# Moving fill parts, row-maximum scores and denominators between the steps of an attention stage, and one DMA ahead in a queue

## The reference, cut to what matters

```
B, T, D = x.shape                       # 2, 1024, 512; H = 16 heads, d = 32
q1, q2 = split(x @ Wq1), split(x @ Wq2)
k,  v  = split(x @ Wk),  split(x @ Wv)
q  = concatenate([q1, q2], axis=1)      # 32 query heads over 16 key heads
scores = einsum('bhqd,bhkd->bhqk', q, repeat(k, 2)) / sqrt(d)
scores = where(causal, scores, finfo.min)
p  = softmax(scores)
y  = einsum('bhqk,bhkd->bhqd', p, repeat(v, 2))
y1, y2 = y[:, :H], y[:, H:]
y  = y1 - sigmoid(x @ Wlam) * y2
return y.reshape(B, T, D) @ Wo
```

## Time and profile before

| what | us |
|---|---|
| median of 3 runs (2035.85 to 2036.71) | 2036.25 |
| the profiled execution, its own time | 2035.62 |
| its span, first to last instruction | 2033.8 |
| TensorE busy | 1964.0 |
| VectorE busy | 1304.9 |
| GpSimd busy | 864.2 |
| ScalarE busy | 827.8 |

### The profile page before, as it was taken

One profiled execution on the slowest core, in us unless ns is written; L12 is line 12 of the kernel. 1 busy time (PEld: TensorE's weight loads), 2 busy tenths in 40 slices (PEclk: granted clock), 3 DMA queues, 4 the chain that ended last, 5 costly groups with the idle time before them and its releaser, 6 DMA issues.

```text
span 2033.8 us, 36873 instructions
## 1 busy us (share of the span) xinstructions
PE 1964.0 (97%) x15184; PEld 834.6 (41%) x15184; DVE 1304.9 (64%) x2610; ACT 827.8 (41%) x1259; POOL 864.2 (42%) x451
## 2 busy tenths in 40 slices
PE   7998999899999999999999999999998899899999
PEld 3444444444444443333333333333333334344444
DVE  5868686836847456566666666666667635774644
ACT  4435353425444322444444443444434452543431
POOL 3756575800000000667767677777776740000000
PEclk9999999999999999999999999999999999999999
DMA  8111010030000003000101000010000211000001
GB/s 243 32 31 35 28 42 27 21 140 1 1 1 1 1 8 70 23 17 23 22 21 24 12 24 16 22 23 22 2 23 6 62 34 42 1 1 22 21 1 42
DMA packets 71592, 60.21 MB, mean 30 GB/s; under 512 B 37312, under 2 KB 55744, under 8 KB 71168
## 3 DMA queue, kind: packets, MB, share of 16 engines
q1 hardware_dynamic: 64512, 45.27, 7.8%
q10 hardware_dynamic: 6912, 12.59, 2.1%
HBM read 43.02 MB, written 10.62 MB: 26 GB/s over the span
## 4 chain that ended last, share of the span: by engine, by line
PE 53%; DVE 5%; POOL 2%; issue 1%; ACT 1%; DMA 0%; SPq 0%; DVEq 0%; POOLq 0%; ACTq 0%
PE psum L128 9%; PE psum L1231 8%; PE psum L1321 8%; PE psum L1379 6%; PE psum L1362 6%; PE psum L152 5%; PE psum L1271 3%; PE psum L1335 2%; PE psum L1358 2%; POOL b_totals L1628 1%; PE psum L1349 1%; DVE b_maxima L1701 1%; PE psum L1280 1%; DVE psum L1709 1%; DVE x L1767 0%
## 5 line engine op out<-in xcount | busy, mean ns | idle before, releaser
L1628 POOL TENSOR_TENSOR b_totals<-b_totals,b_probs 128x2048 f32<-128x2048 f32 (+3 forms) x100 | 323.9, 3239 | 151.3 <-ACT b_probs L1546 147.7
L1709 DVE CUSTOM_DVE_ANT_0 psum<-psum,b_rest 128x512 f32<-128x512 f32 (+3 forms) x512 | 233.5, 525 | 173.4 <-PE psum L1321 173.3
L447 PE MATMUL psum<-hT,a_win 128*128 128x512 f32 x640 | 292.5, 600 | 0.8 <-ACT hT L574 0.8
L128 PE MATMUL psum<-hT,b_early 128*128 128x512 f16 x1024 | 227.0, 381 | 9.8 <-DVE b_middle L214 6.9
L128 PE MATMUL psum<-hT,W 128*128 128x512 f16 x1024 | 227.5, 382 | 3.6 <-DVE a_win L214 3.6
L1546 ACT ACTIVATE b_probs<-psum 128x1024 f32<-128x1024 f32 (+3 forms) x214 | 153.6, 768 | 150.9 <-PE psum L1362 150.8
L1701 DVE TENSOR_REDUCE b_maxima<-psum 128x2 f32<-128x1024 f32 x128 | 150.8, 1220 | 85.5 <-PE psum L1321 85.2
L1628 POOL TENSOR_TENSOR b_totals<-b_totals,b_rest 128x2048 f32<-128x2048 f32 (+3 forms) x50 | 162.0, 3240 | 68.3 <-ACT b_rest L1546 66.5
L447 PEld LDWEIGHTS psum<-hT,a_win 128*128 128x128 f32 x640 | 120.1, 192 | 130.4 <-issue 129.2
L128 PEld LDWEIGHTS psum<-hT,b_early 128*128 128x128 bf16 x1024 | 99.9, 98 | 133.6 <-DVE b_middle L214 8.8
L128 PEld LDWEIGHTS psum<-hT,W 128*128 128x128 bf16 x1024 | 100.7, 99 | 126.3 <-issue 7.0
(11 more groups left out here) (244 smaller groups left out, 3429.5 us busy)
## 6 DMA issues: line engine op xcount, KB each, us to landing
a_parts<-in_w_guT ACTq DMA_DIRECT2D x32, 256.0 KB, 2.8
ternary<-W SPq DMA_DIRECT2D x1, 6144.0 KB, 18.2
a_win<-in_w_inT SPq DMA_DIRECT2D x20, 256.0 KB, 7.2
a_parts<-in_w_pT ACTq DMA_DIRECT2D x16, 256.0 KB, 2.6
b_down<-lam_rows SPq DMA_DIRECT2D x32, 128.0 KB, 2.7
b_early<-ternary SPq DMA_DIRECT2D x8, 512.0 KB, 8.6
out<-x SPq DMA_DIRECT2D x16, 256.0 KB, 2.6
x<-in_x SPq DMA_DIRECT2D x3, 1024.0 KB, 7.9
```

What stands on the lines that cost most here:

```text
L128: last = pe.matmul(self.bank[self.up_bank(i, m) + part], self.gu[:, k * 2 * HID + col:k * 2 * HID + col + P], self.hT[:, at:at + BLK], sta ...
L447: last = pe.matmul(ring(s, j), win[:, at:at + P], core["hT"][:, (i * KT + k) * BLK:(i * KT + k + 1) * BLK], start=(k == 0), stop=(k == KT ...
L1628: pool.tensor_tensor(acc, acc, held(u, s)[:, :, off:BLK], ALU.add).then_inc(summed, 1)
L1709: last = dve.tensor_tensor_reduce(scores, scores, row_mask[:, BLK - width:BLK], 1.0, -3e38, ALU.add, ALU.max, maxima[u % 2][:, at:at + 1])
```

## The change

- A step has three places, of which place 0 always comes ahead of `row`, and 1 and 2 behind it. The parts of a job are listed one by one, so they need not be neighbours.
- `FIRST_ROW` is 0: the nine portions of `row` are at steps 0 to 8, and their order is another.
- Key and query parts stand at (0,1) to (3,2); the second projection's parts from (4,1) to (8,2). Both `den` come at place 0, of steps 2 and 4 (before: behind the row of steps 2 and 5). `neg` is at step 9 (before: 10), and VectorE's `negate` one step earlier.
- At step 4 ScalarE copies `den` ahead of the weighed values.
- SP issues `turn_keys(0)` ahead of the loads of wv and of turn 1's weights.

```diff
-ROWS = [[(0, 0), (2, 0)], [(4, 0)], [(1, 0), (5, 1)], [(5, 0)], [(6, 0)], [(4, 1), (6, 1)], [(3, 0)], [(7, 1)], [(7, 0)]]
+ROWS = [[(0, 0), (2, 0)], [(1, 0), (5, 1)], [(4, 1), (6, 1)], [(3, 0)], [(4, 0)], [(5, 0)], [(6, 0)], [(7, 1)], [(7, 0)]]
-FIRST_ROW = 1
+FIRST_ROW = 0
...
-FIRST_HALF = {(0, 0): "k0", (2, 1): "den1", (3, 0): "k1", (5, 1): "den0", (6, 0): "q0", (8, 0): "q1", (10, 1): "neg0"}
+FILLS = [{(0, 1): "k0", (0, 2): "k0", (1, 1): "k0", (1, 2): "k0", (2, 0): "den1", (2, 1): "k1", (2, 2): "k1",
+          (3, 1): "k1", (3, 2): "k1", (4, 0): "den0", (4, 1): "q0", (5, 1): "q0", (5, 2): "q0", (6, 1): "q0",
+          (7, 1): "q1", (7, 2): "q1", (8, 1): "q1", (8, 2): "q1", (9, 0): "neg0"}]
...
-FILL_BEFORE_ROWS = (0, 4)
-NORM_AT = {(3, 0): 0, (4, 0): 1, (6, 0): 2, (7, 0): 3}
+NORM_AT = {(2, 1): 0, (3, 1): 1, (6, 1): 2, (7, 1): 3}
...
+            turn_keys(0)
             sp.dma_start(wv_all[:, :].rearrange("p (k n) -> p k n", k=KT),
...
-            turn_keys(0)
...
-                    if i in FILL_BEFORE_ROWS and (u, i, 0) in PART_AT:
+                    if (u, i, 0) in PART_AT:
                         fill(*PART_AT[u, i, 0])
                     if row_in(u, i):
                         row(*row_in(u, i))
-                    if i not in FILL_BEFORE_ROWS and (u, i, 0) in PART_AT:
-                        fill(*PART_AT[u, i, 0])
-                    if (u, i, 1) in PART_AT:
-                        fill(*PART_AT[u, i, 1])
+                    for place in (1, 2):
+                        if (u, i, place) in PART_AT:
+                            fill(*PART_AT[u, i, place])
...
-                    if i == CHUNK_LAST[0] + 1:
-                        weigh_out(u, 0)
...
+                            if place == 0 and i == CHUNK_LAST[0] + 1:
+                                weigh_out(u, 0)
...
-                    if i == NS - 2 and u + 1 < UNITS:
+                    if i == NS - 3 and u + 1 < UNITS:
                         negate(u + 1)
```

More of the change, by code:

```diff
@@ L1 @@
+import itertools
 from contextlib import ExitStack
@@ L925 @@
 PARTS = {"k": KT, "q": KT, "v": KT}
-FIRST_HALF = {(0, 0): "k0", (2, 1): "den1", (3, 0): "k1", (5, 1): "den0", (6, 0): "q0", (8, 0): "q1", (10, 1): "neg0"}
-SECOND_HALF = {(0, 0): "q0", (2, 1): "den1", (3, 0): "q1", (5, 1): "den0", (6, 0): "v0", (8, 0): "v1", (10, 1): "neg0"}
+FILLS = [{(0, 1): "k0", (0, 2): "k0", (1, 1): "k0", (1, 2): "k0", (2, 0): "den1", (2, 1): "k1", (2, 2): "k1",
+          (3, 1): "k1", (3, 2): "k1", (4, 0): "den0", (4, 1): "q0", (5, 1): "q0", (5, 2): "q0", (6, 1): "q0",
+          (7, 1): "q1", (7, 2): "q1", (8, 1): "q1", (8, 2): "q1", (9, 0): "neg0"}]
+FILLS.append({at: {"k0": "q0", "k1": "q1", "q0": "v0", "q1": "v1"}.get(name, name) for at, name in FILLS[0].items()})
 OUT_AT = [{9: 2, 11: 3}, {10: 0, 11: 1}]
-FILL_BEFORE_ROWS = (0, 4)
-NORM_AT = {(3, 0): 0, (4, 0): 1, (6, 0): 2, (7, 0): 3}
+NORM_AT = {(2, 1): 0, (3, 1): 1, (6, 1): 2, (7, 1): 3}
 INVERT_AT = {3: (1, 0), 4: (1, 1), 6: (0, 0), 7: (0, 1)}
@@ L940, in job_from @@
         return {(1, 1): ("den", u - 1, 1), (4, 0): ("den", u, 0)}.get((i, place))
-    name = (SECOND_HALF if w else FIRST_HALF).get((i, place), "none0")
+    name = FILLS[w].get((i, place), "none0")
     kind, n, last = name[:-1], int(name[-1]), r == TURNS - 1
@@ L964 @@
 EPILOGUE_BANKS = [7]
-PLACES = [(u, i, place) for u in range(UNITS) for i in range(NS) for place in range(2)]
 PART_AT, ENDING, STEADY = {}, {}, []
-for _n, _at in enumerate(PLACES):
+for _at in itertools.product(range(UNITS), range(NS), range(3)):
     _job = job_from(*_at)
     if _job:
[L971 to L976, removed]
+        if not STEADY or STEADY[-1] != _job:
+            STEADY.append(_job)
+            _part = 0
+        PART_AT[_at] = (_job, _part)
+        _part += 1
+        if _part == PARTS.get(_job[0], 1):
+            ENDING[_at] = _job
 JOBS = PROLOGUE + STEADY + EPILOGUE
@@ L1563, in _ @@
                         act.activation(e_root[:, :], e_var[:, :], ACT.Sqrt).then_inc(early_root, 1)
-                    for place in range(2):
+                    for place in range(3):
                         if (u, i, place) in ENDING:
                             copy_out(ENDING[u, i, place])
+                        if place == 0 and i == CHUNK_LAST[0] + 1:
+                            weigh_out(u, 0)
             weigh_out(UNITS - 1, 1)
@@ L1819, in _ @@
                 for i in range(NS):
-                    if u == UNITS - 2 and NORM_AT.get((i + 1, 0), 2) < 2:
-                        early_turn(0, NORM_AT[i + 1, 0])
-                    if i == NS - 2 and u + 1 < UNITS:
+                    if u == UNITS - 2 and NORM_AT.get((i + 1, 1), 2) < 2:
+                        early_turn(0, NORM_AT[i + 1, 1])
+                    if i == NS - 3 and u + 1 < UNITS:
                         negate(u + 1)
```

## The result

| | before | after |
|---|---|---|
| median, us | 2036.48 (2035.85 to 2038.46) | 2085.01 (2082.49 to 2088.01) |
| ratio, 95% interval | | 1.0238 (1.0226 to 1.0250) |
| the profiled execution, its own time | 2035.62 | 2088.01 |
| its span | 2033.8 | 2086.1 |

The change costs 48.5 us, 2.4%. The forecast was 2073 with a range of 2044 to 2090: the sign and the range held, the size was 12 us short. The median lies outside the 2060 to 2082 that the prediction gave its own mechanism and at the lower edge of the 2085 to 2097 that it gave the rival on the clock.

What follows compares the result with a forecast made beforehand. TensorE bounds on average, GpSimd's list from step 5 on. Even units 5.4, odd 18.0, bias waits 7.2, units 0 and 1 5.4, units 13 to 15 1.1, prologue -0.4: +36.7 us, 2073 us, range 2044 to 2090.

Steps and rivals of the forecast that it cites:

- the rival on the clock: Odd units: the 2.4 us wait at step 10 brings a 1.2 GHz stretch, 1.7 to 3.5 us each; 2085 to 2097, chance 0.17.
- Two bounds: TensorE bounds on average; from step 5 on GpSimd's list is a second bound, with 0.54 us to spare in odd units.
- the rival at 2044: TensorE is the only bound, GpSimd's list slips into its idle time and no wait on it appears: +8 us, chance 0.1.
- Steps 0 to 4: First part of each unit: grows by 4.15 us to 25.7, 3.0 of it work moved from steps 5 to 11.
- the row at step 0: Start of each unit: the row waits 0.9 us for the first exponential, in each of 15 units.
- the wait in step 3's scores: Step 3: this wait goes, 0.17 us shown and taken as 0.35; 0.15 is lost again at step 3's portion.
- the wait at step 4: Fill part behind `den` at step 4 waits for ScalarE to copy bank 7: 0.45 us lost.
- GpSimd's product: Odd units: last product ready 27.6 us after step 5 began, TensorE there at 25.2, so step 10's output waits 2.4.
- The bias wait at the odd start: GpSimd has the bias 31.4 us after the even unit's step 5, so the next odd unit starts waiting 1.2 us.
- Even units: Steps 5 to 11 take 29.9 us, as outputs wait for nothing of this; each even unit grows by 0.9.
- Unit 13: Its output waits for GpSimd as in any odd unit: +3.0 us, between +1 and +5.
- Unit 1: Bias wait 2.6 us instead of 1.30, net +1.3, and +3.6 with the step-0 to 4 effects.

## Why the prediction was right, and where its size was off

**Two bounds: right.** GpSimd at 41% of the span decided the time, since its list does not begin before step 5. The rule of the highest occupancy that the rival at 2044 drew on (the Trainium skill, Perfetto Trace Analysis, Identifying the Most-Contended Engine), taken over the whole span, would have passed it by; the measurement decides against using it so here. The rival's own number came true where its condition was made true: with GpSimd's products and bias early enough the kernel ran in 2044.8. That it agrees so closely is in part luck: units 2 to 12 grew by 0.5 (even) and 0.7 (odd), not 0.85, and unit 14 by 0.5, where the sum had -2.5.

**Steps 0 to 4: right to 0.2 us.** They take 25.50 (1160.49 to 1185.99), forecast 25.7. The single terms: the row at step 0 cost 0.97 (2.30 from the short `weigh` to the fill part, against 0.24 and 1.09 for the two where nothing waits), forecast 0.9; the wait in step 3's scores went, and its row waits 0.15, as forecast; the wait at step 4 shows as 0.28, forecast 0.45.

**GpSimd's product: right.** The output of step 10 starts 27.5 us after step 5 (1154.21 - 1126.72), forecast 27.6, with a wait of 2.35, forecast 2.4. The bias wait at the odd start is 1.39, forecast 1.2. Even units were forecast 0.4 too long, at 29.9 us from step 5 on; they took 29.7.

**The clock: the step that failed.** I set against that rival that TensorE is fully busy ahead of the wait, and that 1.73 us in the prologue were followed by nothing. Neither weighed: TensorE was busy for 10.00 of 10.00 us ahead of the wait in unit 5, and the 1.2 GHz came all the same, in each odd unit from 1 to 11; and what followed 1.73 us said nothing of a wait of 2.35. The rival's mechanism was right and its price too high in those units: 1.19 us each, by the kernel that fills the wait, not 1.7 to 3.5. That the range held all the same is owed to having been stretched over the cheaper half of this rival. By starts, beside the kernel with GpSimd's list reordered, the output takes 2.67 us instead of 1.72 and the scores behind it 1.43 instead of 0.79, but the last `weigh` 0.46 instead of 0.80, since the second output no longer waits for x: a third of a microsecond is given back. In the five odd units 3 to 11 that makes 6.0 us, as much as the 5.7 by which they passed the forecast.

**Unit 13: mis-sized.** I gave it the wait of any odd unit, +4.2 with its bias, and it grew by 12.2. Two waits on TensorE's timeline after (answering to the earlier trace rows, whose wait was 0.46):

```profile
1591.60 0.40 PE L1360 MATMUL psum<-b_last_bias,b_ones_b 32*128 32x512 bf16 x2 [1.41 <-DVE b_maxima L1702]
...
1623.45 3.64 PE L1337 MATMUL psum<-b_wo,b_down 128*32 128x512 f32 x16 [3.06 <-POOL b_down L1651]
```

The first is for the maxima in step 5; from 1591.9 on the clock is at 1.2 GHz for 13.7 us. Steps 5 to 7, which have no fill parts in this unit, take 20.7 us by starts, against 14.9 before and 16.8 with GpSimd's list reordered, where only 3.4 us of them are at 1.2 GHz. The second wait is followed by another 6.8 us. With the waits at step 10 filled this unit takes 61.11: the stretch behind its second wait is gone, which the matmuls explain, but the first one is 3.4 us long too, and up to there this unit's work is the same. The first wait, 1.41 us, stands in five traces with the same work of TensorE in steps 5 to 7: 13.7 us at 1.2 GHz lie behind it in the changed kernel, 3.4 with GpSimd's list reordered and with the waits filled, none where only the product was moved and where a fill part stands ahead of step 0's row. The stretch of steps 5 to 7 in the changed kernel, and where only the product was moved:

```profile
1588.95:1609.68 20.73, 19.32 (x90) 0.67 0.00 1
...
1572.22:1587.37 15.15, 13.23 (x88) 1.00 0.01 1
```

So these steps take 15.15 us at the full clock, 16.75 with 3.4 us of the lower one and 20.73 with 13.7: the first stretch costs 5.6 us. The rest of the unit is 2.4 us shorter with the wait at step 10 filled, which prices the second. Together that is the 8.0 us by which the unit passed its forecast; the mis-sized term is the clock's here too. Why the first stretch has another length in each of these traces was not settled. The four executions of the changed kernel lie in two pairs, 2082.5 and 2082.9 us at a mean clock of 0.989, 2087.1 and 2088.0 at 0.986, and the profiled one is the slowest of them. So its 13.7 us may well not stand in the faster pair, which was not traced.

**Unit 1: 1.9 short.** Its wait for the bias is 2.41, forecast 2.6 (before 1.30):

```profile
868.47 0.63 PE L1360 MATMUL psum<-b_last_bias,b_ones_b 32*128 32x512 bf16 x4 [2.41 <-POOL b_last_bias L1614]
```

Two stretches of 3.4 us at 1.2 GHz lie in this unit, from 868.2 and from 922.8 on. The kernel that fills the wait at step 10 keeps the first and loses the second: this unit takes 61.64 there instead of 62.95, so the second costs 1.3. For the first there is an estimate: steps 0 to 4 take 29.11, 26.70 without the wait of 2.41; where only the product was moved the wait is 1.71, no stretch follows, and they take 27.34, 25.63 without it: 1.1 us. Together they more than cover the 1.9 (the wait itself was forecast 0.2 too long).

**The rest.** Unit 14 gained 1.1, forecast 2.5, within its bounds. The prologue's first row waits 0.91 for ScalarE's copy instead of 1.73 for the DMA, 0.8 us less, where I took 1.0; the prologue as a whole gained 0.5, forecast 0.4, and the other 0.4 of the table's -0.93 lie ahead of the stage. None of this decides anything.

## What to carry to other kernels

Before work is moved on the busiest engine, look at every other engine's list stretch by stretch: where one runs without a gap towards something that the busiest engine waits for, its spare time there (0.54 us here) is what may be taken away in front of it, whatever its share of the whole. When such a list turns out to be late, put in it first what others wait for: two moved calls gave back 40 of 48.5 us. And price a wait with what follows it: 2.35 us of waiting cost 1.2 us more in a slower clock.

## What the runs showed of the hardware that was not expected

- One wait of 2.35 us, with TensorE busy for all of the 10 us ahead of it, was followed by 3.4 us at 1.2 GHz in each of the odd units 3 to 11, 116 us apart. The waits of 1.36 to 1.40 us at the starts of these units were not followed by one, and neither was one of 1.71 us at the start of unit 1 (only the product moved).
- Behind one and the same wait of 1.41 us, in step 5 of unit 13, five traces show 13.7, 3.4, 3.4, 0 and 0 us at 1.2 GHz.
- Matmuls whose result nobody reads, put into the wait of 2.35 us, kept the clock at 1.00 and made the kernel 8.2 us faster.
- GpSimd's wide sum (128x2048, f32) took 4.50 to 4.58 us, at the median 4.55, in all ten traces, in either order of its list.
